# A two-layer sequence kernel (Mamba, then attention): SiLU as one ScalarE function, GpSimd's scan pairs in place in SBUF, 20 and 12 readouts, and the first attention group's start inside Mamba's end

## What is computed

```python
# layer 0, DI = 1024 channels, N = 16 states
xn = layernorm(x) * (1 + scale) + shift          # scale, shift, gate = ada(silu(c))
x_in, z = split(xn @ in_proj)
u  = silu(conv4(x_in) + conv_b)                  # depthwise, 4 taps
dt_r, B, C = split(u @ x_proj)
dt = softplus(dt_r @ dt_proj + dt_b)
h[t] = h[t-1] * exp(dt[t] * A) + (dt[t] * u[t]) * B[t]     # per channel and state
y[t] = sum_n h[t, n] * C[t, n]
y  = (y + u * D) * silu(z)
x1 = x + gate * (y @ out_proj)
# layer 1, 16 heads of 32
xn = layernorm(x1); q, k, v = xn @ Wq + bq, xn @ Wk + bk, xn @ Wv + bv
k, v = masked(k), masked(v); q = softmax(q over 32 features); k = softmax(k over tokens)
y  = q @ (k^T v)                                 # per head
out = x1 + silu(film(layernorm(y))) @ Wo + bo
```

## Time and profile before

| | |
|---|---|
| median of 3 runs | 4806.68 us (4803.45 to 4808.08) |
| the profiled execution's own time | 4803.31 us |
| its span, first to last instruction | 4801.3 us |
| mean granted TensorE clock in it | 0.982 |
| busy share: PE, DVE, ACT, POOL | 90%, 86%, 68%, 82% |
| stages, from the timeline | setup and head to about 118 us, Mamba to about 3616 us, attention from 3619 us |

### The profile page before, as it was taken

The page is one execution under the profiler, slowest core; times in us unless marked ns, Lnnn a source line. Parts: engine busy times, 40 slices in busy tenths (PEclk is TensorE's granted clock), DMA queues, the critical chain, the costliest instruction groups (busy, mean ns, idle before and its releaser), DMA issues. The chain is left out here.

```text
span 4801.3 us, 74789 instructions
## 1 busy us (share of the span) xinstructions
PE 4343.3 (90%) x21344; PEld 3077.7 (64%) x21344; DVE 4110.9 (86%) x5035; ACT 3262.8 (68%) x7813; POOL 3932.5 (82%) x1828
## 2 busy tenths in 40 slices
PE   7898889988898989888889989999878999999998
PEld 4666666666666666666666666666655666666655
DVE  2999999999999999999999999999995665665664
ACT  2888788887887888788878878888762333333332
POOL 1999999999999999999999999999993333343332
PEclk9999999999999999999999999999989999999999
DMA  5111111111111111111111111111122232222321
GB/s 200 41 45 47 45 46 47 45 58 54 62 45 45 45 47 45 48 45 52 60 55 53 45 45 47 45 47 45 45 84 90 92 100 87 98 88 87 104 82 46
DMA packets 122574, 301.03 MB, mean 63 GB/s; under 512 B 15409, under 2 KB 20785, under 8 KB 121714
## 3 DMA queue, kind: packets, MB, share of 16 engines
q1 hardware_dynamic: 120610, 288.52, 17.5%
q10 hardware_dynamic: 1616, 8.39, 0.4%
HBM read 245.35 MB, written 51.51 MB: 62 GB/s over the span
## 5 line engine op out<-in xcount | busy, mean ns | idle before, releaser
L787 POOL TENSOR_TENSOR dbu<-du,bc 128x1024 f32<-128x1024 f32 x1024 | 2453.9, 2488 | 103.1 <-DMA bc<-b_scratch 94.2
L491 ACT ACTIVATE dA<-dt,c_A 128x256 f32<-128x256 f32 x4096 | 1698.6, 463 | 520.0 <-DVE hC L655 498.7
L744 DVE TENSOR_TENSOR_SCAN dA<-dA,dbu 128x512 f32<-128x512 f32 x1088 | 1288.6, 1212 | 21.8 <-ACT dA L491 18.3
L744 DVE TENSOR_TENSOR_SCAN hS<-dA,dbu 128x512 f32<-128x512 f32 x960 | 1157.5, 1212 | 108.5 <-ACT dA L491 50.2
L798 POOL TENSOR_TENSOR hS<-hS,bc 128x1024 f32<-128x1024 f32 x480 | 1193.4, 2486 | 15.9 <-DVE hS L744 15.9
L325 PE MATMUL Y<-c_ident,hC 128*128 128x128 f32 x4352 | 584.2, 278 | 159.4 <-DVE hC L655 159.2
L325 PEld LDWEIGHTS Y<-c_ident,hC 128*128 128x128 f32 x4352 | 500.4, 142 | 296.4 <-DVE hC L655 216.4
L655 DVE TENSOR_TENSOR hC<-dA,bc 128x1024 f32<-128x1024 f32 x544 | 653.1, 1201 | 0.0
L325 PE MATMUL Y<-c_ident,hS 128*128 128x128 f32 x3840 | 510.1, 277 | 4.7 <-POOL hS L798 4.7
L390 PE MATMUL side<-xin,c_conv_w 128*128 128x256 f32 x2048 | 500.7, 379 | 0.7 <-DVE zs L676 0.7
L366 PE MATMUL side<-sh_weights,sh_tile 128*128 128x512 f32 x1024 | 501.1, 608 | 0.0
(11 more groups left out here) (132 smaller groups left out, 5460.2 us busy)
## 6 DMA issues: line engine op xcount, KB each, us to landing
bc<-b_scratch SPq DMA_DIRECT2D x256, 512.0 KB, 3.7
sh_tile<-in_x SPq DMA_DIRECT2D x64, 512.0 KB, 6.1
o_scratch<-oS SPq DMA_DIRECT2D x64, 256.0 KB, 2.0
sh_tile<-o_scratch SPq DMA_DIRECT2D x32, 512.0 KB, 4.7
sh_tile<-gate_scratch SPq DMA_DIRECT2D x32, 512.0 KB, 5.7
x_scratch<-p_x_in SPq DMA_DIRECT2D x32, 512.0 KB, 3.2
p_xr<-x_scratch SPq DMA_DIRECT2D x32, 512.0 KB, 6.8
out<-p_xr SPq DMA_DIRECT2D x32, 512.0 KB, 2.9
```

Of the source, the lines that this page charges most:

```text
L491: last = act.activation(dA[:, q % A_RING, e, :], dt[j % 2][:, e, :], ACT.Exp, scale=C["A"][:, 2 * j + e, n:n + 1])
L744: dve.tensor_tensor_scan(out.rearrange("p e t -> p (e t)"), dA[:, q % A_RING, :, :].rearrange("p e t -> p (e t)"), dbu[(q // 2) % B_RING][ ...
L787: gps.tensor_tensor(dbu[p % B_RING][:, :, :, :], du[j % 2][:, :, :].unsqueeze(1).broadcast_to([P, 2, 2, GT]), bc[:, 0, n:n + 2, :].unsquee ...
```

## The change

1. **SiLU as one function.** Z and CV use ACT's `Silu` straight from PSUM (`soft`, L557 and L564 after): Z writes `zs`, CV writes `u`, with no DVE step. `Silu` is in another set of functions than exponential and logarithm, so `take_functions` (L510) loads a set at each switch. The Z and CV of a group are gathered in four `BURSTS`, at units 6, 22, 38 and 58; each burst is one load of the SiLU set, three activations and one load back.
2. **dt.** The DVE step of softplus now writes `dt` in SBUF (`step`), `du` is `dt * u` (`step_times_u`, both in SBUF), and ACT only sets the first columns to 1e30 afterwards (`set_far`).
3. **G pairs in place in SBUF.** `home(q)` gives a G pair's slot `hS`: ACT writes the decays there, the scan reads them there and writes back there. Only D pairs use PSUM, as a ring of two pairs (`E_RING = 2`). `S_RING` goes from 3 to 4 and `C_RING` from 3 to 4.
4. **20/12 readouts.** `KINDS`: each row has 5 D and 3 G pairs, so a group has 20 D and 12 G.
5. **Z** is computed per row `j` (256 columns, both sequences), with 32 matmuls of 256 columns in place of 16 of 512.
6. **The first attention group.** At Mamba's end POOL multiplies o by gate and adds x, DVE and ACT compute its layernorm; the result waits in `sh_tile`. The attention block starts with its transposes. Column constants are loaded earlier, and the wait for the last store of `o` moves from Mamba's end to the attention block's SP queue.
7. All tables of units are new.

```diff
-KINDS = ["GGDGDGDD", "GGDGDGDD", "GGDGDGDD", "GDGDDGDD"]
+KINDS = ["GDGDDGDD", "GDGDDGDD", "GDGDDGDD", "GDGDDGDD"]
-D_ACC = {4: [9, 12, 17, 18], 5: [8, 10, 12, 16, 18]}
-G_ACC = {4: [8, 11, 14, 18], 3: [9, 11, 17]}
+D_ACC = {4: [10, 14, 14, 18], 5: [9, 9, 14, 18, 18]}
+G_ACC = {4: [8, 9, 12, 19], 3: [8, 12, 17]}
...
+BURSTS = [
+    (6, [("Z", 1, 0), ("CV", 1, 1)]),
+    (22, [("CV", 2, 1), ("Z", 2, 0)]),
+    (38, [("Z", 3, 0), ("CV", 3, 1)]),
+    (58, [("CV", 0, 2), ("Z", 0, 1)]),
 ]
...
-YZ_AT = [20, 36, 52, 69]
-YT_AT = [21, 38, 54, 70]
-YF_AT = [23, 37, 56, 70]
+YZ_AT = [18, 36, 52, 66]
+YT_AT = [21, 37, 53, 68]
+YF_AT = [22, 38, 56, 70]
...
-A_RING = 4
-C_RING = 3
-S_RING = 3
+E_RING = 2
+C_RING = 4
+S_RING = 4
...
+    def home(q):
+
+        j, p, half = q // NST, q % NST // 2, q % 2
         if KINDS[j][p] == "D":
-            wait(eng, hcD_done, go * ND + (D_BASE[j] + D_PAIRS[j].index(p) + 1))
+            return dA[:, 2 * E_SLOT[D_BASE[j] + D_PAIRS[j].index(p)] + half, :, :]
+        return hS[S_SLOT[G_BASE[j] + G_PAIRS[j].index(p)]][:, half, :, :]
...
-            last = act.activation(dA[:, q % A_RING, e, :], dt[j % 2][:, e, :], ACT.Exp, scale=C["A"][:, 2 * j + e, n:n + 1])
+            last = act.activation(home(q)[:, e, :], dt[j % 2][:, e, :], ACT.Exp, scale=C["A"][:, 2 * j + e, n:n + 1])
...
+            if kind == "Z":
+                take_functions(SILU)
                 wait(act, filled[kind], nth(kind, j, own))
+                wait(act, yz_done, own * 4 + j - 1)
+                act.activation(zs[j % 2][:, :, :].rearrange("p b c -> p (b c)"), src[:, :], ACT.Silu).then_inc(zs_done, 1)
+            elif kind == "CV":
+                take_functions(SILU)
+                wait(act, filled[kind], nth(kind, j, own))
+                wait(act, du_done, own * 4 - 8 + (j + 1))
+                wait(act, filled["XP"], own - 1)
+                for e in range(2):
+                    last = act.activation(u[par][:, 2 * j + e, :], src[:, e * GT:(e + 1) * GT], ACT.Silu,
+                                          bias=C["cb"][:, 2 * j + e:2 * j + e + 1])
...
+                    states = home(q).rearrange("p e t -> p (e t)")
+                    dve.tensor_tensor_scan(states, states,
                                            dbu[(q // 2) % B_RING][:, q % 2, :, :].rearrange("p e t -> p (e t)"),
                                            0.0, ALU.mult, ALU.add).then_inc(scan_done, 1)
...
+            dve.scalar_tensor_tensor(dt[j % 2][:, :, :].rearrange("p e t -> p (e t)"), src[:, :], 0.0, tmp[:, :], ALU.max, ALU.add).then_inc(dt_done, 1)
...
-            dve.tensor_tensor(du[j % 2][:, :, :].rearrange("p e t -> p (e t)"), src[:, :],
-                              u[par][:, 2 * j:2 * j + 2, :].rearrange("p e t -> p (e t)"), ALU.mult).then_inc(du_done, 1)
+            dve.tensor_tensor(du[j % 2][:, :, :], dt[j % 2][:, :, :], u[par][:, 2 * j:2 * j + 2, :], ALU.mult).then_inc(du_done, 1)
...
+        gps.wait_ge(edge["first_in"], 48)
+        x0, o_in, g_in = tiles_of(shared)[4:]
+        gps.tensor_tensor(o_in[:, :, :], o_in[:, :, :], g_in[:, :, :], ALU.mult).then_inc(gated0, 1)
+        gps.wait_ge(gated0, 1)
+        gps.tensor_tensor(x0[:, :, :], o_in[:, :, :], x0[:, :, :], ALU.add).then_inc(x1_done0, 1)
```

More of the change, by code:

```diff
@@ L364, in piece @@
             if kind == "Z":
-                b, hf = Z_BLOCK[j]
-                last = pe.matmul(out[:, :], xnF[par][:, part, b * P:(b + 1) * P],
-                                 W["in"][:, part, DI + hf * D:DI + (hf + 1) * D], start=(part == 0), stop=(part == KD - 1))
+                for k in two:
+                    last = pe.matmul(out[:, half * 2 * P:(half + 1) * 2 * P], xnF[par][:, k, half * P:(half + 1) * P],
+                                     W["in"][:, k, DI + j * 2 * P:DI + (j + 1) * 2 * P], start=(k == 0), stop=(k == KD - 1))
             elif kind == "O":
@@ L370, in piece @@
                     wait(pe, yzf_done, own * 4 + (part // 2 + 1))
-                last = pe.matmul(out[:, :], yzF[part // 2][par if part < 4 else 0][:, part % 2, j, :], W["out"][:, part, :], start=(part == 0), stop=(part == KI - 1))
+                last = pe.matmul(out[:, :], yzF[part // 2][par if part < 2 else 0][:, part % 2, j, :], W["out"][:, part, :], start=(part == 0), stop=(part == KI - 1))
             elif kind == "XN":
@@ L510, in simple @@
             elif kind == "O":
+                if last and j == 0:
+                    act.wait_ge(st_done0, 1)
+                    act.activation(lnv[:, :], mv[:, :, 1], ACT.Ln, bias=C["eps"][:, 0:1]).then_inc(ln_done0, 1)
+                    act.wait_ge(ln_done0, 1)
+                    act.activation(rstd[:, :], lnv[:, :], ACT.Exp, scale=-0.5).then_inc(rstd_done0, 1)
                 wait(act, o_stored[j], 16 * own)
@@ new lines, in softplus @@
+        def softplus(step, j, src, own):
+            take_functions(LOG_EXP)
+            if step == 0:
+                wait(act, filled["DT"], nth("DT", j, own))
+                wait(act, dt_done, own * 4 + j)
+                act.activation(tmp[:, :], src[:, :], ACT.Abs).then_inc(abs_done, 1)
+            elif step == 1:
+                wait(act, abs_done, own * 4 + (j + 1))
+                act.activation(tmp[:, :], tmp[:, :], ACT.Exp, scale=-1.0).then_inc(exp_done, 1)
+            else:
+                wait(act, exp_done, own * 4 + (j + 1))
+                act.activation(tmp[:, :], tmp[:, :], ACT.Ln, bias=1.0).then_inc(log_done, 1)
@@ L768, in body @@
                     last.then_inc(stats_done, 1)
[L769 to L775 removed]
+                for (kind, j, d, end, bk, off), of, go in side:
+                    if q == end + DT_AFTER - off:
+                        step(j, bank[bk], go + d)
+                    if q == end + DU_AFTER - off:
+                        step_times_u(j, go + d, (of + d) % 2)
+        over_groups(dve, body)
+        x0, o_in, g_in = tiles_of(shared)[4:]
+        dve.wait_ge(x1_done0, 1)
+        for b in range(GB):
+            dve.bn_stats(stats[:, b, :], x0[:, b, :]).then_inc(bn_done0, 1)
+        dve.wait_ge(bn_done0, GB)
+        for b in range(GB):
+            last = dve.bn_aggr(mv[:, b, :], stats[:, b, :])
+        last.then_inc(st_done0, 1)
+        dve.wait_ge(rstd_done0, 1)
+        for b in range(GB):
+            dve.tensor_scalar(g_in[:, b, :], x0[:, b, :], mv[:, b, 0:1], rstd[:, b:b + 1], ALU.subtract, ALU.mult)
     @block.gpsimd
@@ L1116, in body @@
             sg, a, c = g + 2, g + 1, g - 1
+            S = S and not (isinstance(g, int) and g == -2)
             if isinstance(g, int) and g == -1:
-                dve.wait_ge(s["w_in"], 16 * 7)
+                dve.wait_ge(edge["cols_in1"], 16 * 3)
             if A:
```

351 lines of the change are left out of this document (158 added, 193 removed).

## The result

| | us |
|---|---|
| before | 4807.38 median of 4 runs (4803.45 to 4811.95) |
| changed | 5469.81 median of 4 runs (5469.05 to 5471.96) |
| ratio | 1.1378, 95% interval [1.1359, 1.1398] |
| forecast | 4684, range 4600 to 5090 |

The change costs 13.8%. The forecast has the wrong sign, and the time lies outside its range. It lies 20 us from the rival that I gave 0.20, GpSimd and DVE taking turns, which was worked out at 5490.

A forecast was written before the change was run, and what follows sets the result against it. POOL was taken to bound Mamba at 109.0 us a group; DVE's 102.3 plus 3.5 of stalls make 105.8. Savings of 102, 18 (transition) and 3 (head) sum to 123, giving 4684 us, range 4600 to 5090.

The forecast's parts named there:

- the rival that I gave 0.20: Mamba: GpSimd and DVE exclude each other when DVE's inputs are both SBUF; 5490 us, chance 0.20.
- What bounds the kernel, 109.0 us a group by POOL: Mamba before the change: POOL's 47 instructions at 2.317 us, 108.9, fill the whole group; DVE idles about 4.5.
- Two-SBUF-input scans at 1.12 us and `du` at 0.58: DVE in Mamba: 64 scans at 1.12 us and 4 `du` at 0.58 a group, priced from the trace before.
- exclusive port's arithmetic: Mamba: POOL's 101.9 plus DVE's 29.2 make at least 131 us a group; with full waits 158, or 6350 us.
- Sharing by words: Rival, Mamba: POOL and DVE share the port element by element; 112 to 118 us a group, 4880 to 5080, chance 0.10.
- Bursts at 0.4 us each: Mamba: each of four bursts a group costs DVE 0 to 1.6 us, taken as 0.4, together 1.6.
- bursts of 1.6 to 2 us more than I took: Rival, Mamba: bursts hold DVE longer; 107.8 to 110.2 us a group, 4750 to 4825 us, chance 0.12.
- ACT at 88: ACT in Mamba: stays at about 88 us a group, from 89.2, covered by DVE's 102.
- The sum without the port: Mamba: DVE's 102.3 us a group plus 3.5 of stalls, 105.8.
- Stalls of 3.5 us between two near-equal floors: Mamba: POOL's 101.9 and DVE's 102.3 wait for each other, 3.5 us a group, 1.6 of it bursts.
- Transition -18: Mamba's end to attention's K products: 4.2 us in place of 21.6, 17.4 saved; with PE's clock 18.
- Head -3: Before the first scan: four CV steps lose ACT time, set loads mostly fall into ACT's waits; 0 to 6 us saved, taken as 3.

The follow-up runs named there:

- before_edge: Kernel before with only the transition part added (first attention group's load, gate, sum and layernorm in Mamba's end): 4785.67 us, ratio 0.9966.
- 18/14: before_edge with one readout pair more on DVE, 18 D and 14 G pairs a group: 4811.58 us, ratio 1.0023.
- before_in_place: Kernel before with G pairs' decays scanned in place in SBUF, four slots, PSUM ring of two D pairs, no set loads: 5784.46 us, ratio 1.2043.
- pool_writes: Changed kernel with GpSimd's dbu product replaced by a constant write plus a 4-column product: 4622.51 us (one run).
- psum_source: Changed kernel with only the in-place source undone, all decays in the PSUM ring of four units: 5290.5 us, ratio 1.1021.
- edge_18_14_s4: before_edge with 18 D and 14 G pairs a group and a fourth SBUF slot for G pairs: 4774.00 us, ratio 0.9942.
- psum_no_loads: Changed kernel with decays in the PSUM ring again, Silu replaced by Identity and its set loads removed: 4959.65 us, ratio 1.0331.
- 24/8: Changed kernel with 24 D and 8 G pairs a group in place of 20 and 12: 5095.01 us, ratio 1.0614.

## Why the prediction was wrong, step by step

**What bounds the kernel, 109.0 us a group by POOL: right.** before_edge still has POOL busy 120.00 of 120 us in the same stretch, and 18/14 shortens the group only together with a fourth slot.

**Two-SBUF-input scans at 1.12 us and `du` at 0.58: this is the step that failed.** The forecast case took the distance between starts of scans that read PSUM and used it for scans that don't. Measured: 2273 ns in place of 1212 and 1099 in place of 671, 27.2 us a group that the sum had put at nothing. The counterargument was that a scan asks each input half as often as a readout. It doesn't matter: the engines take turns by whole instructions. The earlier trace rows already showed a DVE instruction that ended 0.15 us behind POOL's end, in another form than the G scan, which ends its full 1.08 behind, and the Trainium skill, SBUF — State Buffer, section Who interferes with whom, stated the rule for two SBUF inputs. The trace after agrees with it, 2273 against 1204 ns. A row, a rule and no row against deserved more than 0.20. That every DVE instruction before had a PSUM input is not quite so: the layernorm's statistics read SBUF alone, but only one tensor.

**The exclusive port's arithmetic: right.** 131 stands against 130.1, 5490 against 5470. It is no lower bound, as "at least" had it: both this group and that of before_in_place lie under their sums, by 1.0 and 2.7 us. Its upper end, 158, assumed a whole POOL instruction of wait for each; the mean wait was 1.07.

**Sharing by words: falsified, but not by the group times alone.** At 0.58 us of POOL a scan, before_in_place would be 108.9 + 30 x 0.58 = 126 us a group; it is 139.8. That price was mis-sized, though: 2048 reads of POOL count both of its inputs, 512 of the scan only one. With both it is 1.16 us a scan, which gives 143.7 and can't be told from taking turns, 142.5. The records tell them apart: a product of four columns, 0.20 us by itself, waits for the end of a whole G scan (pool_writes), and a G scan that finds POOL at work ends 1.08 us after POOL does. Engines that share element by element would not wait like that.

**Bursts at 0.4 us each: right for the changed kernel, and only with its deep rings.** In pool_writes DVE's scans wait 13.7 us in 32 groups for decays. In psum_source the same bursts cost at least 10.3 us a group. I had put the rings' gain "inside the stall"; it is what carries the bursts. So the most natural repair, reading PSUM again, gives back only 179 us of 662. Two figures of the prediction don't follow from their own conditions, though no run turned on them: bursts of 1.6 to 2 us more than I took make 112.2 to 113.8 us a group and not 107.8 to 110.2, and the bound for bursts at 1.6 each is 110.6 and not 108, if the rest of the stall stays.

**ACT at 88: right, by two misses that cancel.** Between the first and the last gating multiply ACT is busy 87.9 us a group, in both kernels. The forecast started from 89.2, read from one stretch, and took 1.3 off. A decay written to SBUF takes 495 ns where one written to PSUM takes 463 (both in the changed kernel); 48 a group make 1.5 us, for which the sum had no term. ACT was off the path, so it cost nothing.

**The sum without the port: right as far as it can be seen.** pool_writes has 103.5 us a group beside the forecast's 105.8, with less work on POOL. It contains DVE's sum of 102.3 and the bursts.

**Stalls of 3.5 us between two near-equal floors: about right, its reason too optimistic.** edge_18_14_s4 has floors of 106.6 and 105.6 and needs 108.7, 2.1 above the higher; edge_18_14 had 3.3. Moving readouts is worth 0.3 us of group there, 2.3 by the floors.

**Transition -18: right in its parts.** 4.2 us and 17.4 saved in the trace of before_edge, 13.7 by its medians; 14.4 in the changed kernel, where PE's clock was lower.

**Head -3: wrong in sign.** The first gating multiply starts at 159.1 and not at 147.7, though it now stands two units earlier. Waits for the port are not it: pool_writes has 158.7. Set loads are 5 us of it (psum_no_loads 153.1, psum_source 158.1), so they did not fall into ACT's waits there as I had assumed. The other 6, which psum_no_loads has with neither set loads nor in-place slots, were not traced.

What stays open: why 24/8 leaves 118.4 rather than 112.9. The rows fit a sum of DVE's waits, but which order would make them fewer wasn't tried.

## What to carry to other kernels

Before a buffer moves from PSUM to SBUF, list for each DVE instruction how many inputs are left in PSUM, and whether GpSimd reads SBUF meanwhile. If a DVE instruction would have none, count its whole time as added to GpSimd's, not beside it, and compare that sum with both engines' own. Undo experiments show pairs: here the harmful part (in place) also carried the useful one (deep rings that hide set loads), so neither alone gives the sign of the whole.
